# A decoder layer on one core: setup work spread over four engines, the first three batches in one list, the last batch's feed-forward in other PSUM banks

## The reference, cut to what matters

```python
x = x + attn(layernorm(x))            # 16 heads of 16; q, k, v and output projections
x = x + xattn(layernorm(x), ctx)      # keys and values from 77 context tokens, with a mask
x = x + ffn(layernorm(x))

def ffn(x):                           # soft mixture: 8 experts x 128 slots = 1024 slots
    xn = rms_norm(x, gamma_x); se = rms_norm(slot_embeds, gamma_slot)
    logits = einsum('bsd,etd->bset', xn, se)
    slots = einsum('bsd,bset->betd', xn, softmax(logits, axis=1))     # over tokens
    processed = gelu(slots @ w1) @ w2                                 # 256 -> 1024 -> 256
    combine = softmax(logits.reshape(b, s, e * t), axis=-1)           # over slots
    return einsum('bnd,bsn->bsd', processed, combine)
```

## Time and profile before

| | |
|---|---|
| median of 3 runs | 2020.74 us (2017.63 to 2021.1) |
| time of the profiled execution | 2018.85 us |
| its span | 2017.0 us |
| PE busy | 1812.1 us (90%) |
| DVE, ACT, POOL busy | 1081.9, 961.5, 418.7 us |
| mean granted clock of PE | 0.947 of full speed |

### The profile page before, as it was taken

The page is one execution under the profiler, slowest core; times in us unless marked ns, Lnnn a source line. Parts: engine busy times, 40 slices in busy tenths (PEclk is TensorE's granted clock), DMA queues, the critical chain, the costliest instruction groups (busy, mean ns, idle before and its releaser), DMA issues.

```text
span 2017.0 us, 41529 instructions
## 1 busy us (share of the span) xinstructions
PE 1812.1 (90%) x16912; PEld 1596.0 (79%) x16912; DVE 1081.9 (54%) x2224; ACT 961.5 (48%) x1688; POOL 418.7 (21%) x349
## 2 busy tenths in 40 slices
PE   2566799999999999999999999999999999998876
PEld 1343688889888888888888888888888888888866
DVE  4333456556565555556565656556565656554422
ACT  2211354555555464555545464555545464555442
POOL 1000111222212221222221222122221222122222
PEclk7565799999999999999999999999999999999889
DMA  4000000000000000000000000000000000000000
GB/s 142 1 8 1 8 1 7 9 7 9 1 15 1 15 1 9 7 7 9 2 14 1 15 1 10 7 7 9 2 14 1 15 2 9 7 1 6 1 6 6
DMA packets 20851, 19.88 MB, mean 10 GB/s; under 512 B 9921, under 2 KB 19777, under 8 KB 20289
## 3 DMA queue, kind: packets, MB, share of 16 engines
q1 hardware_dynamic: 20672, 17.06, 2.9%
HBM read 12.86 MB, written 4.19 MB: 8 GB/s over the span
## 4 chain that ended last, share of the span: by engine, by line
PE 81%; DVE 9%; issue 4%; ACT 3%; SPq 1%; POOL 1%; DMA 0%; POOLq 0%; DVEq 0%; ACTq 0%
PE ps L347 19%; PE ps L348 17%; PE ps L349 17%; PE ps L432 4%; PE ps L469 3%; PE ps L563 2%; PE ps L609 2%; PE ps L647 2%; PE ps L579 1%; PE ps L452 1%; PE ps L544 1%; PE ps L499 1%; PE ps L638 1%; PE ps L389 1%; DVE sl_lo L900 1%
## 5 line engine op out<-in xcount | busy, mean ns | idle before, releaser
L1238 POOL TENSOR_TENSOR h_lo<-h_f,h_hi 128x512 fp32r<-128x512 f32 x256 | 330.4, 1291 | 1186.0 <-DVE h_hi L1110 1186.0
L347 PE MATMUL ps<-w_hi,h_hi 128*128 128x256 f32 x1024 | 304.9, 298 | 32.7 <-issue 22.2
L347 PE MATMUL ps<-sl_hi,w_hi 128*128 128x256 f32 x1024 | 304.2, 297 | 22.0 <-DVE cb_lo L900 21.6
L348 PE MATMUL ps<-w_hi,h_lo 128*128 128x256 f32 x1024 | 292.1, 285 | 0.0
L349 PE MATMUL ps<-w_lo,h_hi 128*128 128x256 f32 x1024 | 292.0, 285 | 0.0
L348 PE MATMUL ps<-sl_hi,w_lo 128*128 128x256 f32 x1024 | 290.8, 284 | 0.0
L349 PE MATMUL ps<-sl_lo,w_hi 128*128 128x256 f32 x1024 | 290.7, 284 | 0.0
L1110 DVE CAST h_hi<-h_f 128x512 fp32r<-128x512 f32 x256 | 132.2, 516 | 241.0 <-ACT h_f L860 240.9
L347 PEld LDWEIGHTS ps<-w_hi,h_hi 128*128 128x128 f32 x1024 | 198.2, 194 | 62.5 <-issue 51.1
L977 DVE TENSOR_REDUCE mx<-ps 128x8 f32<-128x2048 f32 x64 | 146.4, 2288 | 151.9 <-PE ps L432 151.9
L860 ACT ACTIVATE h_f<-ps 128x512 f32<-128x512 f32 x256 | 152.4, 596 | 156.5 <-PE ps L349 156.0
(11 more groups left out here) (193 smaller groups left out, 4141.5 us busy)
## 6 DMA issues: line engine op xcount, KB each, us to landing
x<-in_x SPq DMA_DIRECT2D x16, 256.0 KB, 2.7
out<-acc SPq DMA_DIRECT2D x16, 256.0 KB, 2.2
g_w<-in_w SPq DMA_DIRECT2D x2, 1024.0 KB, 6.1
cx<-in_ctxT SPq DMA_DIRECT2D x16, 77.0 KB, 2.0
...
mk_i<-in_mask SPq DMA_DIRECT2D x16, 38.5 KB
```

The source lines that it names most:

```text
L347: te.matmul(o, lhs[0], rhs[0], start=first, stop=False)
L348: te.matmul(o, lhs[1], rhs[0], start=False, stop=False)
L1238: Q_.tensor_tensor(h_lo[:, part, :], h_f[:, part, :], h_hi[:, part, :].bitcast(f32), ALU.subtract)\
```

## The change

The loop's body stays as it is. Ahead of it, `FIRST` and two rounds of `ORDER` become one list per engine, `START`, whose entries carry the batch (`c1.scores.0`). Behind it, the round without `c` and `LAST` become `FINISH` (batches as -1, -2, -3). `MISC_START`, `QUAD_START`, `MISC_FINISH` and `QUAD_FINISH` list the users of the banks in the new order, for the waits. In the setup:

- the bias columns become a step on DVE, `columns`, after the first transposed x; ACT and POOL wait for biases only where they use them;
- w1's gamma is applied while it is copied (ACT) and subtracted (DVE), so the pass over the staged w1 goes;
- the squares of the slot embeddings go from DVE to ACT, their scaling and w2's `lo` from DVE to POOL; `se_t` goes, since `se_hi` and `se_lo` read PSUM;
- `lo.2`, `lo.3`, `hi.4`, `se_hi.1`, `se_lo.1`, `se_transp.1` stand among the steps of batches 1 and 0;
- g_se is staged where `pt2` lies, and SP issues wq2, g_se, gam, w1 and w2 ahead of wkv2, the context and the 32 pieces of wo and wo2.

For batch 15, `hidden` uses banks 1 to 4 (one for each q), `comb` bank 0, and the combine weights lie in `xa_hi`, `xa_lo`.

```diff
-FIRST = dict(
+START = dict(
     pe="""
-        c.xt.1 c.q c.k c.v c.scores.0 c.mt.0 c.shifted.0 c.pv.0 s.se_transp.0 c.scores.1 s.se_transp.1 c.mt.1
-        c.shifted.1 c.scores.2 c.pv.1 c.tr.0 c.ob.0 c.mt.2 c.shifted.2 c.scores.3 c.pv.2 c.mt.3 c.shifted.3 c.pv.3
-        c.tr.1 c.ob.1 c.oproj
+        c0.xt.1 c0.q c0.k c0.v c0.scores.0 c0.mt.0 c0.shifted.0 c0.scores.1 c0.pv.0 c0.mt.1 c0.shifted.1 c0.scores.2
+        c0.pv.1 c0.tr.0 c0.ob.0 c0.mt.2 c0.shifted.2 s0.se_transp.0 c0.scores.3 c0.pv.2 c0.mt.3 c0.shifted.3 c0.pv.3
...
+        m0.hidden.0.1 d1.xt.2 m0.hidden.0.2 c2.xt.1 m0.hidden.0.3 m0.lt.1 d1.kv c2.q c2.k d1.q2 c2.v m0.dispatch.1
...
+        c0.rstd.1 s0.se_scale c0.bias.1 d0.rstd.2 c1.rstd.1 c1.bias.1 d0.bias.2 s0.lo.4 d0.rstd.3 d1.rstd.2 c2.rstd.1
...
+        m-1.comb.0 m-1.outer.0.1 m-1.hidden.1.0 m-1.hidden.1.1 m-1.dispatch.2 m-1.hidden.1.2 m-1.hidden.1.3
+        m-1.slots.2 m-1.comb.1 m-1.lt.3 m-1.combine.0 m-1.hidden.2.0 m-1.outer.1.0 m-1.outer.1.1 m-1.hidden.2.1
+        m-1.dispatch.3 m-1.hidden.2.2 m-1.hidden.2.3 m-1.slots.3 m-1.comb.2 m-1.combine.1 m-1.hidden.3.0
...
+def run_list(steps, order):
+
+    for entry in order.split():
+        head, name, *k = entry.split(".")
+        steps[name](int(head[1:]) % B, *(int(i) for i in k))
...
 def program(engine, handle, steps):
 
-    run(engine, steps, FIRST, c=0, s=0)
-    run(engine, steps, c=1, d=0)
-    run(engine, steps, c=2, d=1, m=0)
+    run_list(steps, START[engine])
     with handle.Fori(1, B - 2) as b:
         run(engine, steps, c=b + 2, d=b + 1, m=b, l=b - 1)
-    run(engine, steps, d=B - 1, m=B - 2, l=B - 3)
-    run(engine, steps, LAST, m=B - 1, l=B - 2)
+    run_list(steps, FINISH[engine])
 
 
...
-        pt2 = sb("pt2", [CTX, R, 2, S])
+        r_pt2 = region(8 * KB)
+        pt2 = at("pt2", [CTX, R, 2, S], f32, r_pt2)
...
+        def last_batch(b):
+
+            return isinstance(b, int) and b == B - 1
+
+        def hidden_bank(b, q):
+
+            return 1 + q if last_batch(b) else 6 - q % 2
+
+        def comb_bank(b):
+
+            return 0 if last_batch(b) else 6
+
+        def comb_tile(b):
+
+            return (xa_hi, xa_lo) if last_batch(b) else (cb_hi, cb_lo)
...
+                        pe.wait_ge(s["i_slo"], 2)
+                        pe.wait_ge(s["i_lo"], 4)
+                        pe.wait_ge(s["i_w2lo"], 1)
...
             def hi(_, n):
 
                 name = WEIGHTS[n]
                 act.wait_ge(s["i_" + name], 16)
+                src, (hi, _) = once(name)
                 if name == "w1":
-                    act.wait_ge(s["i_w1g"], 1)
-                src, (hi, _) = once(name)
-                copy(hi, src).then_inc(s["i_hi"], 1)
-
-            def se_hi(_):
-                act.wait_ge(s["i_sg"], 2)
-                copy(W["se"][0][:, :, :], se_t[:, :, :]).then_inc(s["i_shi"], 1)
-
-            act.wait_ge(s["i_cols"], 1)
+                    act.wait_ge(s["i_gam"], 16)
+                    for dk in range(ND):
+                        last = nc.scalar.activation(hi[:, dk, :], src[:, dk, :], ACT.Identity, scale=gam[:, 0, dk:dk + 1])
...
+            def se_squares(_):
+
+                act.wait_ge(s["i_se"], 16)
+                for e in range(NS):
+                    last = nc.scalar.activation(se_sq[:, e, :], g_se[:, e, :], ACT.Square, accum_out=se_ss[:, e:e + 1])
+                last.then_inc(s["i_st"], 1)
+
+            def se_hi(_, dk):
+                act.wait_ge(s["i_sps"], dk + 1)
+                act.wait_ge(s["i_gxs"], 1)
+                nc.scalar.activation(W["se"][0][:, dk, :], ps[:, 5:7, :].rearrange("p u n -> p (u n)"),
+                                     ACT.Identity, scale=gxs[:, dk:dk + 1]).then_inc(s["i_shi"], 1)
+
...
             def lo(_, n):
 
                 name = WEIGHTS[n]
                 dve.wait_ge(s["i_hi"], n + 1)
                 src, (hi, low) = once(name)
-                minus(low, src, hi).then_inc(s["i_lo"], 1)
+                if name == "w1":
+                    for dk in range(ND):
+                        last = V.scalar_tensor_tensor(low[:, dk, :], src[:, dk, :], gam[:, 0, dk:dk + 1],
+                                                      hi[:, dk, :].bitcast(f32), ALU.mult, ALU.subtract)
+                else:
+                    last = minus(low, src, hi)
+                last.then_inc(s["i_lo"], 1)
 
...
+            def se_lo(_, dk):
+                dve.wait_ge(s["i_shi"], dk + 1)
+                V.scalar_tensor_tensor(W["se"][1][:, dk, :], ps[:, 5:7, :].rearrange("p u n -> p (u n)"),
+                                       gxs[:, dk:dk + 1], W["se"][0][:, dk, :].bitcast(f32), ALU.mult, ALU.subtract)\
+                    .then_inc(s["i_slo"], 1)
...
+                pool.wait_ge(s["i_sr"], 4)
+                Q_.tensor_tensor(g_se[:, :, :], g_se[:, :, :], se_sc[:, :].unsqueeze(2).broadcast_to([P, NS, D]), ALU.mult)\
+                    .then_inc(s["i_xn"], 1)
+
+            def lo(_, n):
+
+                pool.wait_ge(s["i_hi"], n + 1)
+                src, (hi, low) = once(WEIGHTS[n])
+                Q_.tensor_tensor(low, src, hi.bitcast(f32), ALU.subtract).then_inc(s["i_w2lo"], 1)
+
...
+            load("wq2", stage["wq2"][:, :, :])
+            sp.dma_start(g_se[:, :, :], t_in["se"].rearrange("(e p) d -> p e d", p=P)).then_inc(s["i_se"], 16)
+            sp.dma_start(gam[:, :, :], t_in["gam"]).then_inc(s["i_gam"], 16)
+            load("w1", stage["w1"][:, :, :])
+            load("w2", stage["w2"][:, :, :])
+            load("wkv2", W["wkv2"][:, :, :])
```

More of the change, by code:

```diff
@@ new lines @@
+        c1.xo.1 d0.od2.1 s0.se_hi.1 c1.od.0 c1.mh.2 c1.ex.2 s0.hi.4 c1.xo.2 c1.mh.3 c1.ex.3 c1.xo.3 d0.xt.3
+        d0.logits.0 d0.logits.1 d0.logits.2 d0.logits.3 c1.od.1 m0.ed.0 m0.ds.0 m0.sl.0 m0.ge.0.0 d1.xt.2 m0.ge.0.1
+        m0.ge.0.2 c2.xt.1 m0.ge.0.3 c2.q m0.ed.1 d1.q2 m0.ec.0 m0.ds.1 m0.cb.0 m0.sl.1 d1.mh2.0 d1.ex2.0 d1.xo2.0
+        c2.mh.0 m0.pr.0 c2.ex.0 m0.ge.1.0 c2.xo.0 m0.ge.1.1 m0.ge.1.2 d1.od2.0 m0.ge.1.3 d1.mh2.1 m0.ed.2 d1.ex2.1
+        m0.ds.2 m0.ec.1 d1.xo2.1 c2.mh.1 c2.ex.1 m0.sl.2 m0.cb.1 c2.xo.1 m0.ec.2 d1.od2.1 m0.ge.2.0 m0.pr.1 m0.ge.2.1
@@ L713, in combine @@
                     for e in range(2):
-                        last = three(ps[:, 7, t * D:(t + 1) * D], both(CB, full, e, slice(t * P, t * P + P)),
+                        last = three(ps[:, 7, t * D:(t + 1) * D], both(comb_tile(b), full, e, slice(t * P, t * P + P)),
                                      both(PR, full, e), e == 0, e == 1)
@@ L753, in q_step @@
                 act.wait_ge(s["q_ps"], nth("q_ps", a, 1))
+                if not later(a):
+                    act.wait_ge(s["i_cols"], 1)
                 for c in range(C):
@@ L797, in ex2 @@
                 act.wait_ge(s["st2_ps"], nth("st2_ps", a, c + 1))
+                if not c and not later(a):
+                    act.wait_ge(s["i_sps"], 2)
                 if c:
@@ L1117, in cb @@
                 dve.wait_ge(s["cb_hi"], nth("cb_hi", b, c + 1))
-                minus(cb_lo[:, :, :], halves(6), cb_hi[:, :, :]).then_inc(s["cb_lo"], 1)
+                hi, low = comb_tile(b)
+                minus(low[:, :, :], halves(comb_bank(b)), hi[:, :, :]).then_inc(s["cb_lo"], 1)
             def acc_step(b, c):
```

258 lines of the change are left out of this document (160 added, 98 removed).

## The result

The changed kernel takes 1947.1 us in the median (1943.0 to 1953.1, 4 runs), where the kernel before took 2019.2 beside it (2016.2 to 2021.1, 4 runs). The ratio is 0.9647, with a 95% interval of 0.9618 to 0.9676. The forecast was 1946. The profiled execution of after took 1943.01 us, with a span of 1941.2.

What follows compares the result with a forecast made beforehand. TensorE (PE) was taken to bound the loop, whose 1467.6 us stay, leaving 549 us outside it to shorten. The sum was 2018.85 - 28 - 2 - 5 - 38 = 1945.85, say 1946 us, range 1936 to 1956 (chance 0.55).

Steps and rivals of the forecast that it cites:

- Setup and batch 0: Before the loop, setup and batch 0 alone: earlier start and less setup work ahead save 28 us, bounds 24 to 29.5.
- the wall: Batch 0, DVE: w1's scaling and three lo parts stand ahead of quad 0's mx; it starts 18.9 us earlier.
- the squares: Batch 0: slot-embedding squares, now on ACT ahead of quad 0's ex, take 4.4 us; ex ends at 31.4.
- Batches 1 and 0: Round after batch 0: reordered chain of score groups gains 2 us, bounds 8 gained to 5 lost.
- rival 2: Setup moved into batches 1 and 0 sits on their chain, no full-round gain: plus 10, 1956 us; chance 0.13.
- The first full round: Last round before the loop: half of PE's 9.7 us idle time goes, minus 5 us, bounds 0 and 10.
- The loop: Loop body, unchanged with its waits on every engine: its 1467.6 us stay.
- The last two rounds: After the loop: new banks and order remove PE's waits, 173 us instead of 210.9, minus 38, bounds 25 to 42.
- ACT (1): Last rounds: ACT becomes the bound, its single order holding PE; half of the 38 returns, 1965 us; chance 0.15.
- Only batch 0 gaining (4): Whole change: inferred waits are not those of shared banks, only batch 0 gains, about 1991 us; chance 0.05.
- The low clock at the end (5): Last two rounds: clock falls to 1.2 GHz, adding 118 us if all low, 2064 us; chance 0.01.
- Rival 3: Batches 1 and 0 become dense enough for the high clock, gaining 15 us: 1931 us; chance 0.09.

Runs made afterwards that it cites:

- w1_first: Changed kernel with the copies and rests of wq2 and w1 put back ahead of the first score group, new DMA order kept: 1954.7 us, ratio 0.966.
- w1_first_old_dma: Changed kernel with the wq2 and w1 copies and rests back ahead of the first score group, and the old DMA order too: 1969.6 us, ratio 0.973.
- start_only: Changed kernel with the last two rounds in their old order and old shared banks: 1981.8 us, ratio 0.982.
- new_banks_old_order: Changed kernel with the last two rounds in the old order but batch 15's new banks kept: 1974.1 us, ratio 0.977.
- old_round_new_last: Changed kernel with only the round before the last in the old order, new order and banks for batch 15's feed-forward: 1948.5 us, ratio 0.963.
- fixes: Changed kernel with the squares moved behind ex of quad 0, and se_lo.1 and the third statistics behind mx of quad 3 of batch 1: 1947.2 us, ratio 0.962.
- start_rounds: Changed kernel with new batch 0 and spread setup, but the two rounds behind it in the loop's order: 1947.4 us, ratio 0.965.

## Why the prediction was right, step by step

Against the profiled execution the five terms were off by minus 3.5, minus 0.3, plus 0.9, plus 2.0 and minus 1.9 us (minus where it came out faster), minus 2.8 together. That the median lies 1 us from the forecast is luck, both in how these terms balance and in the profiled execution being the fastest of four; a forecast good to some 5 us is what the terms bear out.

**Setup and batch 0** (minus 28, bounds 24 to 29.5; measured minus 31.5). `mx` of quad 0 started at 20.59 (20.9 forecast), so the wall and the start were right, and w1_first and w1_first_old_dma show its parts. The step that was mis-sized is the squares: "eight activations with an accumulator, 0.50 each plus some 0.05, make 4.4 us". They took 3.2:

```profile
24.22 0.41 ACT L1015 ACTIVATE se_sq<-g_se 128x256 f32<-128x256 f32 x1
24.53 0.19 ACT L1015 ACTIVATION_READ_ACCUMULATOR se_sq<-g_se 128x1 f32 x1
24.62 0.41 ACT L1015 ACTIVATE se_sq<-g_se 128x256 f32<-128x256 f32 x1
...
27.45 1.88 ACT L885 ACTIVATE pt<-ps 128x2048 f32<-128x2048 f32 x1
```

The distance from one to the next is 0.40, and `ex` ended at 29.33, not 31.4. Of these 2 us, GpSimd's scaling beside `md` took 1.6 back, so `sh` of quad 1 came at 36.62 (37.4 forecast). Quads 2 and 3 took 24.2 us where the sum had 13.9 + 10.95 + 0.55, and from `sh` of quad 3 to the addition it was 13.3 (60.80 to 74.13) where the kernel before had 14.7 (90.89 to 105.59). The clock was 0.84 from 58 to 66, around the last quad, where the kernel before had 0.50 through its last two quads; that it accounts for these 2.6 us is an argument, not a measurement. The addition was forecast at 77.5 and came at 74.13.

**Batches 1 and 0** (minus 2; measured minus 2.3, and minus 1.7 to 4.4 in the three other kernels with this list). The gain came where the prediction had it: from `mx` of the first self-attention group to `mx` of the second cross-attention group 4.5 us went (14.7 to 10.3; 3.7 forecast), of which the next maximum gave 1.7 back. But between 110.9 and 113.9 us in the kernels with this list, 0.3 us from the forecast is chance. GpSimd took the value chosen, not the other bound:

```profile
158.88 4.51 POOL L1393 TENSOR_TENSOR w_lo<-g_w,w_hi 128x2048 fp32r<-128x2048 f32 x1 [74.78 <-ACT w_hi L856]
163.35 1.02 POOL L1346 TENSOR_TENSOR pw_d<-ve_d,consts 128x4 f32<-128x4 f32 x1
```

5.2 had been taken and 11.1 feared. The Trainium skill's 4.5 us for 2048 elements ("GPSIMD Engine Reference", Elementwise — side-by-side cycle accounting) agrees with the row. PE's wait at `xt.3` named `xo` for 0.5 us, not GpSimd. But "DVE mostly reads PSUM then" overlooked the copy `md` of quad 3, which reads and writes SBUF (the on-chip memory beside PSUM): it took 1.89 us instead of 0.18 and ended 0.04 behind GpSimd's instruction (163.43 and 163.39). So the moved `lo` of w2 does sit on the chain, as rival 2 feared, though at another step and for 1.7 us, not 10.

**The first full round** (minus 5; measured minus 4.1) was right for the wrong reason. The step that failed is "I count half of the idle time gone". Idle time of PE fell from 9.7 to 8.0 us (109.02 less 101.04) and no further. The other 3 us are a stretch of low clock that after happened not to have and start_only, with the same list, had: here of start_only,

```profile
236.00:251.00 15.00, 12.88 (x108) 10.41 (x109) 5.62 (x7) 4.66 (x9) 3.19 (x3) 0.77 0.00 1
```

The same list took 112.1 us in start_only, new_banks_old_order, old_round_new_last, w1_first and fixes. So the term is minus 1, and start_rounds, with the loop's order at 112.9, agrees. What decides whether that stretch is granted the high clock was not found.

**The loop** (0; measured plus 2.0). Its body costs the same, but among the nine kernels without added matmuls it takes 1467.6 to 1478.4, with the stops and, after some of them, a lower clock (0.95 in the 37 us behind the second stop of after, in the pass that took 114.4). "The loop is unchanged" held to 11 us among these nine, and fails by 18 to 29 us where code was added ahead of it.

**The last two rounds** (minus 38; measured minus 39.9). The round without self-attention took 90.4 (91 forecast), the last stretch 80.5 (80), and the 2 us put in for overlooked waits were not needed. The waits came as listed: at the start `h_lo` 2.2, `sl_lo` 1.0, `ds_lo` 0.6 (4 us forecast in all), in the middle, from 1880 to 1922, a single wait of 0.3, at the end 1.8 for `h_lo` and 1.4 for `pr_lo` (1.6 and 1.65). What the prediction did not separate is how much hangs on the banks: it said that the idle time exists "because lt, dispatch, comb and hidden share banks 5 and 6". Alone they gave 6.5 of 36 us; the order gives the rest on top of them. This is the step of the prediction that was wrong in its mechanism, and it did not show in the number because banks and order were changed together.

**Rivals.** ACT (1) heads no wait: `od` 0.6 and `h_f` 0.2 us in both rounds. The late setup (2) showed itself only in the copy above. Only batch 0 gaining (4) is refuted by the end's 40 us; start_only shows what such a kernel takes, 1981.8. The low clock at the end (5) didn't come: 1.00 and 0.98. (Its "about a sixth" of low clock in the last stretch before is too little: at 0.89 in the earlier trace rows, between 0.50 and 1.00, it was 22% of the time.) Rival 3's mechanism is real and worth its price, but had to be bought with added matmuls.
